# A pipelined attention kernel on one core: a branch hint on the image loop, and the value matmuls of two key steps issued together

## What is computed

```python
h = group_norm(x, norm_w, norm_b)                  # 8 groups
q, k, v = split(einsum('bchw,oc->bohw', h, qkv_w) + qkv_b)
x = x + proj(softmax(q k^T / sqrt(128)) v)         # 1 head, 1024 x 1024

t = to_tokens(x)                                   # 1024 x 128
sq, sk, rq = heads of ln(t) @ wq_s, @ wk_s, @ wq_r # 8 heads of 16
rv = heads of ln(t) @ wv_r                         # 2 retrieved heads of 16
retrieved = softmax(sq sk^T / 4) rv                # (8, 1024, 2, 16)
gate = softmax over the 2 of (rq . (retrieved @ wk_ret)) / 4
t = t + (sum over the 2 of gate * retrieved) @ w_out

t = t + ln(t) @ dequant_nf4(qidx, scales)^T @ W^T
```

## Time and profile before

| | |
|---|---|
| median of 3 runs | 5834.74 us |
| the three runs | 5835.21, 5830.56, 5834.74 us |
| the profiled execution's own time | 5838.83 us |
| its span, first to last instruction | 5836.5 us |
| busy: PE, DVE, ACT, POOL | 93%, 68%, 59%, 73% |
| mean granted TensorE clock | 0.981 |

### The profile page before, as it was taken

How to read it: one execution, slowest core, us unless ns; L and a number is a source line. 1 busy time by engine, 2 the same in 40 slices (tenths; PEclk the granted TensorE clock), 3 DMA queues, 4 the chain that set the end, 5 groups by cost and what they waited for, 6 DMA issues and landing times.

```text
span 5836.5 us, 99943 instructions
## 1 busy us (share of the span) xinstructions
PE 5436.7 (93%) x30350; PEld 3295.9 (56%) x30350; DVE 3955.0 (68%) x8189; ACT 3470.2 (59%) x6689; POOL 4251.2 (73%) x1109
## 2 busy tenths in 40 slices
PE   5999999999999999999999999999999999999986
PEld 3555555565555555555555555555555555556543
DVE  4776667667676666676667676677766676766763
ACT  2566566656566565666565665666665656665654
POOL 1677777777777777777777777777777777777787
PEclk9999999999999999999999999999999999999998
DMA  1101110111111111111111111111111111101110
GB/s 36 24 26 33 31 38 26 27 34 27 38 26 34 27 34 30 37 26 30 31 27 38 31 29 27 34 30 38 26 34 27 27 37 36 28 24 36 23 33 11
DMA packets 64867, 176.65 MB, mean 30 GB/s; under 512 B 21856, under 2 KB 23264, under 8 KB 64224
## 3 DMA queue, kind: packets, MB, share of 16 engines
q1 hardware_dynamic: 64224, 168.61, 12.3%
HBM read 17.53 MB, written 16.78 MB: 6 GB/s over the span
## 4 chain that ended last, share of the span: by engine, by line
PE 79%; DVE 9%; ACT 5%; issue 4%; POOL 2%; SPq 0%; DMA 0%; DVEq 0%; ACTq 0%; POOLq 0%
PE ps_bank L776 16%; PE ps_u L810 16%; PE ps_bank L799 15%; PE ps_bank L763 7%; PE ps_bank L691 4%; PE ps_bank L679 3%; DVE max_part L1062 3%; DVE max_part L1072 3%; PE ps_bank L747 2%; PE ps_bank L819 2%; PE ps_bank L750 2%; PE ps_bank L749 2%; PE ps_bank L748 2%; POOL p_sum L627 2%; ACT work L963 2%
## 5 line engine op out<-in xcount | busy, mean ns | idle before, releaser
L627 POOL TENSOR_TENSOR p_sum<-p_sum,p 128x2048 f32<-128x2048 f32 x768 | 3509.0, 4569 | 411.4 <-ACT p L982 381.2
L1072 DVE TENSOR_REDUCE max_part<-ps_bank 128x1 f32<-128x512 f32 x4096 | 2613.7, 683 | 1237.9 <-PE ps_bank L776 1224.9
L982 ACT ACTIVATE p<-ps_bank 128x512 f32<-128x512 f32 x4096 | 2283.6, 599 | 1495.3 <-PE ps_bank L799 1482.6
L799 PE MATMUL ps_bank<-q_stack,k_stack 128*128 128x512 f32 x4096 | 1726.3, 438 | 25.1 <-DVE t_front L1096 20.7
L776 PE MATMUL ps_bank<-k_stack,q_stack 96*128 96x512 f32 x4096 | 1594.6, 426 | 25.9 <-DVE max_part L1072 11.2
L776 PEld LDWEIGHTS ps_bank<-k_stack,q_stack 96*128 96x128 f32 x4096 | 777.6, 193 | 687.5 <-DVE max_part L1072 287.2
L627 POOL TENSOR_TENSOR p_sum<-p 128x2048 f32<-128x2048 f32 x128 | 584.3, 4565 | 792.4 <-ACT den_sb L990 731.3
L799 PEld LDWEIGHTS ps_bank<-q_stack,k_stack 128*128 128x128 f32 x4096 | 766.2, 192 | 655.1 <-issue 273.2
L810 PE MATMUL ps_u<-p,rv 128*32 128x512 f32 x8192 | 1114.5, 617 | 19.1 <-ACT u_sb L987 12.2
L763 PEld LDWEIGHTS ps_bank<-v,p 128*128 128x128 f32 x4096 | 494.1, 191 | 17.8 <-issue 2.4
L763 PE MATMUL ps_bank<-v,p 128*128 128x129 f32 x4096 | 498.2, 274 | 1.6 <-ACT p L939 1.6
(11 more groups left out here) (140 smaller groups left out, 4600.2 us busy)
## 6 DMA issues: line engine op xcount, KB each, us to landing
q_stack<-q_hi SPq DMA_DIRECT2D x256, 128.0 KB, 2.4
k_stack<-k_hi SPq DMA_DIRECT2D x512, 64.0 KB, 2.3
x_sb<-in_x SPq DMA_DIRECT2D x32, 512.0 KB, 3.3
t_held<-t_front SPq DMA_DIRECT2D x32, 512.0 KB, 2.9
k_stack<-k_lo SPq DMA_DIRECT2D x256, 64.0 KB, 2.4
q_stack<-q_lo SPq DMA_DIRECT2D x128, 128.0 KB, 2.3
t_core<-t_held SPq DMA_DIRECT2D x32, 512.0 KB, 3.4
out_y<-out_sb SPq DMA_DIRECT2D x32, 512.0 KB, 2.6
```

What stands on the lines that cost most here:

```text
L627: pool.tensor_tensor(p_sum[:, :, :], before, p1[:, step % ring, :, :], ALU.add)\
L799: pe.matmul(out, k_stack[:, head, keys], q_stack[:, head // 2, queries], start=True, stop=True)\
L982: act.activation(p1[:, step % ring, n, :], read_bank(), ACT.Exp, scale=scale1)\
L1072: dve.tensor_reduce(max_part1[:, i, n, half:half + 1], read_bank(), AXIS.X, ALU.max)\
```

## The change

Two edits. First, the loop of `in_order` is opened by another call, which puts a branch prefetch hint at the head of the body on PE, ACT, DVE and POOL; the loop of SP is as it was. Second, `schedule()` places no `values` in odd steps, and in even steps the values of the two steps before, one directly after the other. The body of `sum_values` is the same: each of the two has its own wait and its own semaphore increment.

```diff
@@ schedule() @@
-            behind = ("HEAD", "values", step - 1) if step else ("TAIL", "values", 31)
-            placed.append((VALUES_AT if n else 0.02, behind))
+            if step % 2 == 0:
+                for late in (2, 1):
+                    behind = ("HEAD", "values", step - late) if step else ("TAIL", "values", 32 - late)
+                    placed.append((VALUES_AT if n else 0.02, behind))
@@ in_order() @@
-def in_order(engine, steps, images, stages, banks=None, links=None, first=None):
+def in_order(nc, engine, steps, images, stages, banks=None, links=None, first=None):
...
-    with engine.Fori(1, images - 2) as b:
+    with nc.Fori(1, images - 2, engines=[engine.engine], hint_back_edge=True) as b:
```

More of the change, by code:

```diff
@@ L628, in add_weights @@
                         .then_inc(p1_summed, 1)
-                in_order(pool, steps, images, {"values": add_weights, "norm_group_var": rstd0,
+                in_order(nc, pool, steps, images, {"values": add_weights, "norm_group_var": rstd0,
                                                "ln1_stats": rstd_shift(0), "ln2_stats": rstd_shift(1)})
@@ L857, in tensor_program @@
                 }
-                in_order(pe, steps, images, stages, banks, first=first_of_image)
+                in_order(nc, pe, steps, images, stages, banks, first=first_of_image)
             def scalar_program(act):
@@ L1017, in scalar_program @@
                 }
-                in_order(act, steps, images, stages, banks)
+                in_order(nc, act, steps, images, stages, banks)
             def vector_program(dve):
@@ L1186, in vector_program @@
                 }
-                in_order(dve, steps, images, stages, banks, links)
+                in_order(nc, dve, steps, images, stages, banks, links)
             with nc.Block() as block:
```

## The result

| | before | with the change |
|---|---|---|
| median of 4 runs each | 5833.13 us | 5755.62 us |
| lowest and highest | 5830.56 to 5835.21 | 5747.94 to 5763.73 |
| profiled execution, its span | 5836.5 | 5746.2 |
| mean granted clock | 0.981 | 0.986 |

A forecast was written before the change was run, and what follows sets the result against it. PE, 93% busy, was taken to set the time: 5838.8 us profiled, less 123 for the hint and 129 for the double visits, gave 5587, or 5583 us at the median of runs; range 5528 to 5670.

The forecast's parts named there:

- The branch: At the loop's branch back, the hint removes PE's 3.13 us fetch stall and slow clock: 4.38 us each, 123 us.
- Rival (a): At the loop's branch, the hint does nothing, the head is fetched as late as before: 5706 us, chance 0.08.
- (c): In the loop body, the hinted block displaces sequential fetch and PE misses: 5967 us with three misses, chance 0.03.
- The clock: Behind the branch stall PE runs at 1.2 GHz, 1.45 us more per branch; this goes with the stall.
- The price of a pair: Two visits back to back go into and out of the narrow form once: 0.31 us saved in each of 512.
- What is lost of it: Visits in steps 18, 26 and 28 bring no gain, 3 of 16, leaving 129 us from the double visits.
- Rival (b): Double visits give nothing, as ACT and DVE make PE wait for banks in odd steps: 5712 us, chance 0.08.
- the forecast's slow end: Two thirds of the visits' gain swallowed and half a us left at the branch: 157 us off, 5678.
- The cover of the ring and of POOL: Later values leave ACT's exponentials 1.7 steps instead of 2.7, POOL catches up after three steps: both cost nothing.

The follow-up runs named there:

- e1: The changed kernel with the hint alone, one visit of the values in each step as before the change: 5742.26 us, 0.9844 of before.
- e3: Hint and double visits as in the change, but single visits in steps 9, 10, 17, 18, 21, 22 and 25 to 28: 5636.06 us.
- e2: The changed kernel without the loop hint, double visits alone: 5885.62 us, 1.0082 of before.
- e4: Against e1, double visits only in steps 10, 18, 22, 26 and 28, single visits outside those pairs: 5876.2 us, 1.0073 of before.
- e8: Against e3, `ln1_channels` of step 19 moved to 0.45 of the step; `norm_group_var` slid to the step's head: 5679.1 us.
- e9: Against e3, `ln1_channels` at 0.45 of step 19 and `norm_group_var` kept at that step's end: 5572.05 us, 0.9549 of before.

## Why the prediction was wrong

Of the 252 us, 77 came. Of the 175 us missing, 142 belong to the double visits (129 gained in the forecast, 13 lost between e1 and the change) and 33 to the hint (123 forecast, 90 in e1).

**The branch: right in itself.** The stall of 3.13 us was instruction fetch (q14's packets in step 31 go with it), the hint removes it, L952 and DVE stay hidden behind the double visit, and steps 31 and 0 are 4.65 us shorter. Rival (a) falls by this, and (c) too: no wait without a releaser of this kind stands anywhere else in the body.

**The clock: mis-sized.** 1.45 us a branch, times 28, was read from one branch. In the same trace 20 of the 28 have slow clock behind them; these steps 31 and 0 take 15.2 us together, the other eight 13.3, and 10.3 in e1. So the mean gain of e1, 4.36 us a branch against 4.38 forecast, is in part luck: too many branches were counted, each with too little lost. And "The gap that makes the clock fall goes with it" took this as gained for good. The rows of the forecast had a second wait that could do the same, 74.3 us in 33 pieces for L963, and did not count it as a cause of slow clock. With the branch's gap gone, the clock falls there. With the hint alone about 13 of the 41 us were kept (e1), in the changed kernel 29 ((112.6 - 44.4) x 0.43).

**The price of a pair: right on the mean.** A double visit takes 1.85 us. Between e1 and e3 eleven pairs give 3.4 us an image, 0.31 for each, but singly they lie between 0.01 (13, 14) and 0.89 (3, 4); the fit of the mean is better than the forecast could know.

**What is lost of it: the step that failed.** "I count the visits in steps 18, 26 and 28 as lost, 3 of 16": the term was 129 us gained, and the runs show 30 us lost once the clock is taken out (e2). The stretches were found, steps 17 and 25 to 28 with DVE near 100%, but the wrong price was put on them. A pair is not one saving that PE's wait may swallow. It is a visit of 1.21 us taken out of one step and 0.86 us put into another, and each is worth what its own step's bound makes it worth. Out of a step that DVE or ACT bounds it brings nothing, into one that PE bounds it costs in full. So a lost pair counts +0.86 and not 0, and two more pairs were missed, 9 with 10, where ACT is the bound, and 21 with 22, where the chain through ACT and DVE is. The measured price of a lost pair is the +0.78 to +0.87 of the table, and e4 shows the five alone to cost 134 us. Rival (b) had named waits for the readers in odd steps, but put its floor at zero gain. That the double visit itself starves the readers, its other half, is not what the trace shows: step 26 grows by the two passes and by no wait.

The row that would have said so was in the trace before: in step 25 matmuls start every 0.60 us where the earlier trace rows has 0.23. PE counts as busy there, 5.03 of 5.24 us, because a matmul's duration of 0.49 us runs over most of the distance.

The range was narrower than its own working: the forecast's slow end came out at 5678 us and was set at 5670. That changes nothing here. The cover of the ring and of POOL held: PE's waits for POOL's adds ahead of a `den` are 29.5 us after 27.2.

## What to carry to other kernels

Moving work of the bounding engine from one stretch to another is two edits; price the taking out and the putting in separately, each by what bounds its own stretch, and read that from the distances between starts, not from busy shares. Work that stands where the engine has to wait anyway is free, and an even spread of it by count is not an even spread of the time. When a stall goes, look for the next one of its kind before booking what hung on it, the clock above all.

## What the runs showed of the hardware

- PE's idle gap at the loop's branch, 3.13 us in each of 28, is gone with a branch prefetch hint, and with it four packets of the instruction queue q14 per branch. What is left is 0.25 us (0.60 us from L786 to L749, of which the four transposes take 0.35).
- A wait of 1.93 us between stretches in which PE was busy was enough for the clock to fall to 1.2 GHz in 24 of 28 images (e1), and in 10 of 28 in the kernel before: in all 8 images that came without slow clock at the branch ahead, and in 2 of the 20 that came with it. Why a fall at the branch spares the wait 104 us later is left open. A wait of 2.29 us did it in 28 of 28 (e8). Without both waits the clock did not fall once inside the loop (e9).
- It can fall without any such wait: in step 25 of e4, in 6 images, PE started a matmul each 0.60 us and stood still for about 0.1 us between two of them, and the clock went to 1.2 GHz.
- Narrow float32 matmuls, four side by side: passes follow each other after 0.43 to 0.45 us without a seam between two visits, and going into the form and out of it costs 0.31 us.
- DVE takes a 128x512 bank each 0.60 us when it is driven, though the mean duration of a reduction is 0.683 us; PE's matmuls then start at exactly that distance.
